# Later turns, copies and second projections, inner values in two parts, and one longer pause per column in a vision tower with a mixture of experts

## The chip, the cores and the metric

The kernel runs on one core of a Trainium2 chip. The metric is the device time of one execution in microseconds, taken as the median of several runs. Engines are named as in the profile: PE is TensorE's matmul stream and PEld its weight loads, DVE is VectorE, ACT is ScalarE, POOL is GpSimd, SP is SyncE, which here only issues DMAs.

## The reference

16 images of 128 x 512 floats are cut into 8 x 8 patches, which makes 1024 tokens of 64 values for each image. Each token is embedded (a 64 x 64 matrix, a bias, a position row), goes through a layer norm and linear attention over 8 heads, and then through a layer norm and 16 experts of which the two best are weighed:

```python
h = _L0_tok_ref(x, W, b, pos_embed)
h = h + _L0_attn_ref(_layernorm(h), Wk, bk, Wq, bq, Wv, bv, Wr, br)
h = h + _L0_ffn_ref(_layernorm(h), gate_w, gate_b, w1, w2, w3)
# the experts, of which the top two count for a token, with weights that sum to one:
h1 = einsum('bsd,edh->bseh', x, w1); h2 = einsum('bsd,edh->bseh', x, w2)   # 64 -> 128 for each expert
hidden = silu(h1) * h2
expert_out = einsum('bseh,eho->bseo', hidden, w3)                          # 128 -> 64
```

All of it is in float32.

## The kernel before

The images are taken as 8 pairs. For a pair, `attend` does the embedding, the attention, the second norm, the choice of experts and the sorting of tokens by expert, cut into stages: a table `PLANS` gives each stage a number k, whole or with a fraction, and `BEGUN` gives the step at which a pair begins (`step_of`). For the experts, POOL scatters the tokens of a pair (twice, once for each of their two experts) as rows of 512 bytes into a DRAM list sorted by expert. The list has 48 tiles of 128 rows, and each tile belongs to one expert. Four tiles are a group, so a pair has 12 groups, and 96 groups g are numbered through all pairs. A group goes through this chain:

- SP loads the rows (`load_rows`), PE turns them (`turn`, four transposes into `turn_ps`), ACT copies them to `rowsT` (also called `turn`, two buffers);
- PE does the first projections (`project_in`, 8 matmuls of 256 columns into `h_ps`, which takes two PSUM banks and has one buffer); the expert of each tile is read into PE registers first (L1144);
- ACT takes the tanh (`activate`), DVE makes the inner values in two steps (`multiply`: `twice`, then `hid`, two buffers);
- PE turns them (`turn_hidden` into `hidT_ps`), ACT copies them (`copy_hidT`, two buffers);
- PE does the second projections (`project_out` into `y_ps`), ACT copies them (`copy_y`, two buffers), SP stores them (`store_y`).

When all rows of a pair are stored, POOL gathers the two rows of each token (`gather`), ACT and DVE weigh and add them (`weigh`, `sum_up`) and SP stores the result.

What sets the order is a loop over steps s that every engine's program has by itself, written out in full. Group g = s - LAG (22) belongs to step s. In step s PE does `project_in(g)`, `turn_hidden(g - 1)`, the stages k of the pairs under way, `turn(g + 1)`, the stages k + 0.5, `project_out(g - 1)` and the stages k + 0.75 (L1174 to L1189). ACT does the stages k, `copy_y(g - 2)`, `activate(g)`, `copy_hidT(g - 1)`, `turn(g + 1)`, the stages k + 0.5 and then the weighing (L643 to L661). DVE does the stages, `multiply(g)`, more stages and sums. Engines wait for each other by counting semaphores only, so one engine may be in another step than the others, but each works its own list strictly in order.

POOL issues 512 indirect DMAs: for each of a pair's 16 columns of 128 tokens two scatters, and later two gathers. A table says in which steps (`SCATTER`, `GATHER`, 6 steps for 16 columns), and at the start of each step POOL waits until PE has turned group g (L526). Ahead of each indirect DMA, `pause` writes 192 zeros per partition into a scratch tile `idle`, and nobody reads them (L477 to L481).

Of the kernel before, what the change touches and what calls it, by code (L numbers as in the profile page):

```python
# [11 lines left out]
ACT = mybir.ActivationFunctionType  # L12
# [50 lines left out]
SCATTER = (16, 22, 29, 43, 56, 69, 82, 95)  # L63
GATHER = (36, 49, 62, 75, 88, 101, 108, 120)
SUMS = [[42 + 14 * m + q for q in range(4)] for m in range(5)] + [[113, 114, 115, 116], [119, 119, 120, 120], [121, 122, 123, 124]]
STORED = 2
# [29 lines left out]

GROUPS_ALL = GROUPS * PAIRS


def vit_kernel(nc, x, tok_w, tok_b, pos, wk, bk, wq, bq, wv, bv, wr, br, gate_w, gate_b, w1, w2, w3, out):  # L100
# [3 lines left out]
    with ExitStack() as ctx:  # L104
# [114 lines left out]

        idle = sb("idle", [P, 192])  # L220
        rows_all = sb("rows_all", [P, 3, GROUP, 2, E])
# [104 lines left out]
        def _(sp):  # L326
# [102 lines left out]
        def _(pool):  # L429
# [53 lines left out]
            def scatter(m, j):  # L483

                n = m % 3
                if j == 0:
                    wait(pool, "place_ready", m + 1)
                    wait(pool, "z_split", m + 1)
                    if m >= 3:
                        wait(pool, "rowsT_ps_ready", GROUPS * (m - 2))  # L490
                    else:
                        pool.wait_ge(rows_zeroed[n], 16)
                for r in range(2):
                    pause()
                    gp.indirect_dma_start(rows_dram[n], bass.IndirectOffsetOnAxis(ap=place[m % RING][:, r, j:j + 1], axis=0),  # L495
                                          z_parts[m % 2][:, j // 2, j % 2, :, :].rearrange("p n e -> p (n e)").bitcast(F32),
                                          None).then_inc(scattered[n], 16)

            def gather(m, j):
# [9 lines left out]
                if j == 0 and apart(m):  # L509
                    wait(pool, "att_ps_ready", 3 * PAIRS)  # L510
                for r in range(2):
                    pause()
                    gp.indirect_dma_start(y_of[r][apart(m)][:, j // 2, j % 2, :], None, y_dram[m % 3],  # L513
                                          bass.IndirectOffsetOnAxis(ap=place[m % RING][:, r, j:j + 1], axis=0)).then_inc(gathered[apart(m)][q], 16)
# [18 lines left out]
        def _(act):  # L533
# [63 lines left out]
            def turn(g):  # L597
                wait(act, "rowsT_ps_ready", g + 1)
                wait(act, "h_done", g - 1)
                sc.activation(rowsT[g % 2][:, :], turn_ps[:, :], ACT.Copy).then_inc(S["rowsT_ready"], 1)  # L600

            def activate(g):
                wait(act, "h_done", g + 1)
                wait(act, "twice_done", g)
                if g == 0:
                    for n in range(3):
                        act.wait_ge(rows_zeroed[n], 16)
                sc.activation(tanh[:, :, :], h_ps[:, :].rearrange("p (j n h) -> p j n h", j=GROUP, n=2)[:, :, 0, :],  # L608
                              ACT.Tanh, scale=0.5).then_inc(S["tanh_done"], 1)

# [32 lines left out]
            for s in range(SPAN):  # L643
                g = s - LAG
                for m, k in steps_at(s):
                    attend(m, k)
                if 0 <= g - 2 < GROUPS_ALL:
                    copy_y(g - 2)
                if 0 <= g < GROUPS_ALL:
                    activate(g)  # L650
                if 0 <= g - 1 < GROUPS_ALL:
                    copy_hidT(g - 1)
                if 0 <= g + 1 < GROUPS_ALL:
                    turn(g + 1)
                for m, k in steps_at(s):
# [8 lines left out]
        def _(dve):  # L664
# [280 lines left out]
            def find_owners(m):  # L945
                wait(dve, "owner_ps_ready", m + 1)
                if m >= 3:
                    wait(dve, "h_done", GROUPS * (m - 2))
                ve.tensor_scalar(owner[m % 3][:, :], sides[second(m)][0:1, 258:258 + TILES], float(EXPERTS - 1), None,
                                 ALU.min).then_inc(S["owner_ready"], 1)  # L950

            def multiply(g):
                wait(dve, "tanh_done", g + 1)
                wait(dve, "hid_done", g)
# [3 lines left out]
                ve.scalar_tensor_tensor(twice[:, :, :], tanh[:, :, :], 1.0, halves[:, :, 0, :], ALU.add, ALU.mult).then_inc(S["twice_done"], 1)  # L958
                wait(dve, "twice_done", g + 1)
                wait(dve, "hidT_ps_ready", g - 1)  # L960
                ve.scalar_tensor_tensor(hid[g % 2][:, :, :], twice[:, :, :], 0.5, halves[:, :, 1, :], ALU.mult, ALU.mult).then_inc(S["hid_done"], 1)  # L961

# [28 lines left out]
        def _(pe):  # L991
# [146 lines left out]
            def project_in(g):  # L1138
# [7 lines left out]
                wait(pe, "rowsT_ready", g + 1)  # L1146
                wait(pe, "hid_done", g)
                for j, e in enumerate(experts[g]):
                    for w, first in ((w_hi, True), (w_lo, False)):
                        mm = te.matmul(h_ps[:, j * 256:(j + 1) * 256], rowsT[g % 2][:, j * P:(j + 1) * P],  # L1150
                                       w[:, bass.ds(e, 1), :, :].rearrange("d a n h -> d (a n h)"), start=first, stop=not first)
                mm.then_inc(S["h_done"], 1)

            def turn_hidden(g):
                wait(pe, "hid_done", g + 1)
                wait(pe, "hidT_ready", g)
# [15 lines left out]
            for s in range(SPAN):  # L1172
# [15 lines left out]
                for m, k in steps_at(s):  # L1188
# [24 lines left out]
```

## Time and profile before

| | |
|---|---|
| median of 3 runs | 1007.12 us (1001.66 to 1008.42) |
| the profiled execution | 997.99 us, span 996.1 us |
| PE, PEld busy | 69%, 57% of the span |
| POOL busy | 66% |
| DVE, ACT busy | 43%, 34% |
| TensorE's granted clock, mean | 0.773 of full |
| POOL's indirect DMAs | 512, 0.95 to 0.99 us each |

Read the shares as means over a start (until about 160 us) in which there are no groups yet, a long middle with attention and groups, a stretch from about 780 us with groups and gathers only, and an end from 941 us in which POOL gathers for the last pair.

### The profile page before, as it was taken

How to read it: one execution, taken by the hardware profiler on the slowest of the kernel's cores; microseconds unless marked ns; L12 is line 12 of the kernel's file. 1: busy time of each engine (PE TensorE's matmuls, PEld its weight loads, DVE VectorE, ACT ScalarE, POOL GpSimd, SP SyncE). 2: the span in 40 equal slices, each digit the busy share in tenths (PEclk: the TensorE clock that was granted, in tenths of full speed). 3: DMA queues.
4: the chain of work that ended last, by engine and by line, in shares of the span. 5: the costliest groups of instructions: out<-in, count | busy, mean ns of one | idle time of the engine just before them, and what ended most of it. 6: DMA issues, size and time to landing. Idle time of an engine off the chain costs nothing.

```text
span 996.1 us, 14389 instructions
## 1 busy us (share of the span) xinstructions
PE 684.5 (69%) x3844; PEld 568.1 (57%) x3844; DVE 427.0 (43%) x1045; ACT 339.2 (34%) x657; POOL 661.8 (66%) x1052
## 2 busy tenths in 40 slices
PE   6866676886778677886777777887659556656500
PEld 3555356765775576565755667577657555545400
DVE  4755534642445544453555264534552221112411
ACT  2231112432342444244443354234432332223611
POOL 1050786848588677848884888757884887586085
PEclk9978767877789878878898787977875767657755
DMA  2991312343321732253335243242422333223221
GB/s 62 169 347 75 102 45 85 91 116 101 88 68 43 173 107 74 60 143 91 104 71 118 81 122 90 48 125 80 108 70 70 92 93 80 69 68 78 58 44 31
DMA packets 168871, 93.20 MB, mean 94 GB/s; under 512 B 99680, under 2 KB 152928, under 8 KB 168800
## 3 DMA queue, kind: packets, MB, share of 16 engines
q1 hardware_dynamic: 151632, 66.71, 25.7%
q0 software_dynamic: 16384, 25.20, 9.3%
q8 instruction: 39, 0.64, 0.3%
q10 hardware_dynamic: 784, 0.39, 0.2%
q14 instruction: 32, 0.26, 0.1%
HBM read 45.06 MB, written 47.19 MB: 93 GB/s over the span
## 4 chain that ended last, share of the span: by engine, by line
PE 41%; another core or an unknown queue 25%; issue 12%; DVE 8%; ACT 6%; POOL 4%; DMA 2%; SPq 0%; ACTq 0%; POOLq 0%; DVEq 0%
PE h_ps L1150 11%; PE y_ps L1167 7%; PE hidT_ps L1160 4%; PE wide_ps L1019 4%; PE turn_ps L1135 4%; POOL sums L513 3%; PE wide_ps L1039 2%; ACT sums L633 1%; ACT hidT_all L616 1%; PE wide_ps L1111 1%; PE side_ps L1086 1%; POOL idle L480 1%; DMA rows_all<-rows_scratch 1%; PE wide_ps L1126 1%
## 5 line engine op out<-in xcount | busy, mean ns | idle before, releaser
L495 POOL DMA_INDIRECT rows_scratch<-z_parts,place x256 | 254.4, 994 | 43.6 <-issue 40.7
L480 POOL MEMSET idle<- 128x192 f32 x512 | 140.2, 274 | 196.4 <-issue 62.9
L513 POOL DMA_INDIRECT sums<-y_scratch,place x224 | 219.0, 978 | 36.6 <-issue 33.3
L1150 PE MATMUL h_ps<-w_hi,rowsT 128*128 x384 | 140.7, 382 | 97.6 <-issue 53.7
L1167 PE MATMUL y_ps<-w_sb,hidT_all 128*128 x768 | 128.5, 320 | 94.5 <-issue 49.8
L1167 PEld LDWEIGHTS y_ps<-w_sb,hidT_all 128*128 128x128 f32 x768 | 118.6, 233 | 113.9 <-issue 113.5
L958 DVE SCALAR_TENSOR_TENSOR twice_y<-tanh,h_ps 128x512 f32<-128x512 f32 x96 | 65.9, 686 | 264.2 <-ACT tanh L608 134.7
L1150 PEld LDWEIGHTS h_ps<-w_hi,rowsT 128*128 128x128 f32 x384 | 97.0, 252 | 113.4 <-issue 112.9
L1150 PE MATMUL h_ps<-w_lo,rowsT 128*128 x384 | 129.8, 352 | 0.0
L600 ACT ACTIVATE rowsT<-turn_ps 128x512 fp32r<-128x512 f32 x96 | 57.5, 599 | 183.3 <-remote 112.8
L608 ACT ACTIVATE tanh<-h_ps 128x512 f32<-128x512 f32 x96 | 57.2, 596 | 164.1 <-remote 78.8
L1150 PEld LDWEIGHTS h_ps<-w_lo,rowsT 128*128 128x128 f32 x384 | 99.9, 260 | 0.1
L1160 PE MATMUL hidT_ps<-ident,hid_all 128*128 128x128 f32 x384 | 81.5, 351 | 1.7 <-issue 1.7
L1135 PE MATMUL turn_ps<-ident,rows_all 128*128 128x128 f32 x384 | 74.3, 323 | 9.6 <-issue 8.4
L621 ACT ACTIVATE twice_y<-y_ps 128x256 f32<-128x256 f32 x96 | 36.7, 383 | 105.4 <-remote 73.4
L1135 PEld LDWEIGHTS turn_ps<-ident,rows_all 128*128 128x128 f32 x384 | 57.9, 172 | 22.3 <-issue 19.7
L961 DVE SCALAR_TENSOR_TENSOR hid_all<-twice_y,h_ps 128x512 f32<-128x512 f32 x96 | 65.9, 686 | 3.3
L616 ACT ACTIVATE hidT_all<-hidT_ps 128x512 f32<-128x512 f32 x96 | 57.2, 596 | 28.5 <-remote 19.1
L1160 PEld LDWEIGHTS hidT_ps<-ident,hid_all 128*128 128x128 f32 x384 | 62.0, 182 | 1.1 <-issue 1.1
L1019 PE MATMUL wide_ps<-w_patch,x_cols 64*128 64x512 f32 x224 | 56.6, 627 | 3.1 <-DVE w_patch L683 3.1
L970 DVE SCALAR_TENSOR_TENSOR sums<-sums,gate 128x64 f32<-128x64 f32 x112 | 24.5, 280 | 78.2 <-ACT sums L633 39.0
L633 ACT ACTIVATE sums<-sums,mean_all,gate 128x64 f32<-128x64 f32 x112 | 39.9, 431 | 39.0 <-DMA sums<-y_scratch,place 39.0
(251 smaller groups left out, 946.3 us busy)
## 6 DMA issues: line engine op xcount, KB each, us to landing
rows_all<-rows_scratch SPq DMA_DIRECT2D x96, 256.0 KB
y_scratch<-twice_y SPq DMA_DIRECT2D x96, 128.0 KB
rows_scratch<-tanh SPq DMA_DIRECT2D x3, 3072.0 KB, 19.4
xi_scratch<-xi SPq DMA_DIRECT2D x16, 256.0 KB
rows_scratch<-z_parts,place POOLq DMA_INDIRECT x256
hx<-xi_scratch SPq DMA_DIRECT2D x14, 256.0 KB
sums<-y_scratch,place POOLq DMA_INDIRECT x224
out<-sums SPq DMA_DIRECT2D x56, 64.0 KB
```

The lines of the kernel that those rows point to most:

```text
L480: gp.memset(idle[:, :], 0.0).then_inc(S["idled"], 1)
L495: gp.indirect_dma_start(rows_dram[n], bass.IndirectOffsetOnAxis(ap=place[m % RING][:, r, j:j + 1], axis=0), z_parts[m % 2][:, j // 2, j % ...
L513: gp.indirect_dma_start(y_of[r][apart(m)][:, j // 2, j % 2, :], None, y_dram[m % 3], bass.IndirectOffsetOnAxis(ap=place[m % RING][:, r, j: ...
L600: sc.activation(rowsT[g % 2][:, :], turn_ps[:, :], ACT.Copy).then_inc(S["rowsT_ready"], 1)
L616: sc.activation(hidT[g % 2][:, :], hidT_ps[:, :], ACT.Copy).then_inc(S["hidT_ready"], 1)
L958: ve.scalar_tensor_tensor(twice[:, :, :], tanh[:, :, :], 1.0, halves[:, :, 0, :], ALU.add, ALU.mult).then_inc(S["twice_done"], 1)
L961: ve.scalar_tensor_tensor(hid[g % 2][:, :, :], twice[:, :, :], 0.5, halves[:, :, 1, :], ALU.mult, ALU.mult).then_inc(S["hid_done"], 1)
L1019: te.matmul(wide_ps[:, b * 512:(b + 1) * 512], x_cols[second(m)][half, j, :], w_patch[half, j, :, :].rearrange("p t e -> p (t e)"), start= ...
L1135: mm = te.transpose(turn_ps[:, j * P:(j + 1) * P], rows[g % 3][:, j, :, :].rearrange("p n e -> p (n e)"), ident[:, :])
L1150: mm = te.matmul(h_ps[:, j * 256:(j + 1) * 256], rowsT[g % 2][:, j * P:(j + 1) * P], w[:, bass.ds(e, 1), :, :].rearrange("d a n h -> d (a ...
L1160: mm = te.transpose(hidT_ps[:, j * P:(j + 1) * P], hid[g % 2][:, j, :], ident[:, :])
L1167: mm = te.matmul(y_ps[:, j * E:(j + 1) * E], hidT[g % 2][:, j * P:(j + 1) * P], w3_sb[:, bass.ds(e, 1), :].rearrange("h a d -> h (a d)"), ...
```

## The change

Six things are changed together. PE turns the rows of group g + 2 instead of g + 1 in a step, and has its second projections of group g - 2 (it was g - 1) ahead of `turn_hidden`, right behind the first ones. ACT begins a step with its three copies, those of `hidT` and `y` a group later than before, and ahead of the stages. Tanh and inner values of a group are made in two halves of two tiles each (`HALVES`), with counts to match, and so are PE's first projections: the second half waits for the second half of the inner values before. SP loads rows three groups ahead and stores three behind. `pause` writes 512 zeros instead of 192 and is called once a column instead of once an indirect DMA. POOL's wait at L526 is not changed in text, but the turn of group g is now done a step earlier. The tables `GATHER` and `SUMS` move some entries by one step.

```diff
-GATHER = (36, 49, 62, 75, 88, 101, 108, 120)
-SUMS = [[42 + 14 * m + q for q in range(4)] for m in range(5)] + [[113, 114, 115, 116], [119, 119, 120, 120], [121, 122, 123, 124]]
+GATHER = (37, 49, 62, 75, 88, 101, 109, 121)
+SUMS = [[42 + 14 * m + q for q in range(4)] for m in range(5)] + [[114, 115, 116, 117], [120, 120, 121, 121], [122, 123, 124, 125]]
+HALVES = (slice(0, GROUP // 2), slice(GROUP // 2, GROUP))
-        idle = sb("idle", [P, 192])
+        idle = sb("idle", [P, 512])
-                if 0 <= g + 2 < GROUPS_ALL:
-                    load_rows(g + 2)
-                if 0 <= g - 2 < GROUPS_ALL:
-                    store_y(g - 2)
+                if 0 <= g + 3 < GROUPS_ALL:
+                    load_rows(g + 3)
+                if 0 <= g - 3 < GROUPS_ALL:
+                    store_y(g - 3)
...
+                pause()
                 for r in range(2):
-                    pause()
                     gp.indirect_dma_start(...)
...
             def activate(g):
-                wait(act, "h_done", g + 1)
-                wait(act, "twice_done", g)
-                sc.activation(tanh[:, :, :], ...)
+                for i, j in enumerate(HALVES):
+                    wait(act, "h_done", 2 * g + i + 1)
+                    wait(act, "twice_done", 2 * g + i - 1)
+                    sc.activation(tanh[:, j, :], ...)
...
                 g = s - LAG
+                if 0 <= g + 1 < GROUPS_ALL:
+                    turn(g + 1)
+                if 0 <= g - 3 < GROUPS_ALL:
+                    copy_y(g - 3)
+                if 0 <= g - 2 < GROUPS_ALL:
+                    copy_hidT(g - 2)
                 for m, k in steps_at(s):
                     attend(m, k)
-                if 0 <= g - 2 < GROUPS_ALL:
-                    copy_y(g - 2)
                 if 0 <= g < GROUPS_ALL:
                     activate(g)
-                if 0 <= g - 1 < GROUPS_ALL:
-                    copy_hidT(g - 1)
-                if 0 <= g + 1 < GROUPS_ALL:
-                    turn(g + 1)
...
             def multiply(g):
+                for i, j in enumerate(HALVES):
+                    wait(dve, "tanh_done", 2 * g + i + 1)
+                    wait(dve, "hid_done", 2 * g + i - 1)
+                    ve.scalar_tensor_tensor(twice[:, j, :], ...)
+                    wait(dve, "twice_done", 2 * g + i + 1)
+                    ve.scalar_tensor_tensor(hid[g % 2][:, j, :], ...)
...
             def project_in(g):
-                wait(pe, "hid_done", g)
-                for j, e in enumerate(experts[g]):
+                for i, half in enumerate(HALVES):
+                    wait(pe, "hid_done", 2 * g + i - 1)
+                    for j in range(half.start, half.stop):
...
                 if 0 <= g < GROUPS_ALL:
                     project_in(g)
+                if 0 <= g - 2 < GROUPS_ALL:
+                    project_out(g - 2)
                 if 0 <= g - 1 < GROUPS_ALL:
                     turn_hidden(g - 1)
                 for m, k in steps_at(s):
                     attend(m, k)
-                if 0 <= g + 1 < GROUPS_ALL:
-                    turn(g + 1)
+                if 0 <= g + 2 < GROUPS_ALL:
+                    turn(g + 2)
                 for m, k in steps_at(s):
                     attend(m, k + 0.5)
-                if 0 <= g - 1 < GROUPS_ALL:
-                    project_out(g - 1)
                 for m, k in steps_at(s):
                     attend(m, k + 0.75)
```

## Rows read from the trace of the kernel before

**Rows 1.** The page, sections 1 and 2: busy time of each engine, and granted clock.

```profile
PE 684.5 (69%) x3844; PEld 568.1 (57%) x3844; DVE 427.0 (43%) x1045; ACT 339.2 (34%) x657; POOL 661.8 (66%) x1052
PEclk9978767877789878878898787977875767657755
```

**Rows 2.** The page, section 4: the chain that ended last, by engine.

```profile
PE 41%; another core or an unknown queue 25%; issue 12%; DVE 8%; ACT 6%; POOL 4%; DMA 2%; SPq 0%; ACTq 0%; POOLq 0%; DVEq 0%
```

**Rows 3.** Stretches: from:to, length; busy PE, PEld, DVE, ACT, POOL; clock, DMA, GB/s.

```profile
547.70:655.90 108.20, 85.43 (x501) 70.33 (x501) 52.60 (x126) 43.16 (x85) 81.33 (x128) 0.82 0.36 94
...
811.70:860.20 48.50, 30.28 (x144) 27.39 (x144) 10.84 (x22) 15.24 (x32) 39.39 (x64) 0.63 0.37 87
915.00:941.00 26.00, 18.98 (x117) 16.54 (x115) 12.00 (x30) 15.17 (x37) 0.00 (x0) 0.83 0.24 61
```

**Rows 4.** Timeline of one group's step without POOL (start, length; idle before it).

```profile
922.72 0.40 PE L1150 MATMUL h_ps<-w_hi,rowsT 128*128 x1 [1.06 <-issue]
...
924.64 0.60 ACT L608 ACTIVATE tanh<-h_ps 128x512 f32<-128x512 f32 x1 [2.16 <-PE h_ps L1150]
...
925.50 0.60 ACT L616 ACTIVATE hidT_all<-hidT_ps 128x512 f32<-128x512 f32 x1 [0.26 <-PE hidT_ps L1160]
...
926.24 1.15 PE L1167 MATMUL y_ps<-w_sb,hidT_all 128*128 x8
...
928.41 0.38 PE L1150 MATMUL h_ps<-w_hi,rowsT 128*128 x1 [1.03 <-issue]
```

**Rows 5.** Timeline of a step with POOL at work.

```profile
841.07 1.10 PE L1167 MATMUL y_ps<-w_sb,hidT_all 128*128 x8 [0.39 <-ACT hidT_all L616]
...
845.70 0.38 ACT L621 ACTIVATE twice_y<-y_ps 128x256 f32<-128x256 f32 x1 [3.03 <-remote]
...
850.03 0.60 ACT L608 ACTIVATE tanh<-h_ps 128x512 f32<-128x512 f32 x1 [3.95 <-remote]
```

**Rows 6.** Waits of the whole span: us in total, times, longest us.

```profile
ACT rowsT L600 <- remote: 112.8, 27, 8.9
ACT tanh L608 <- remote: 78.8, 25, 7.0
ACT twice_y L621 <- remote: 73.4, 19, 6.5
```

**Rows 7.** Groups of instructions: busy us, mean ns of one; idle before them.

```profile
L961 DVE SCALAR_TENSOR_TENSOR hid_all<-twice_y,h_ps 128x512 f32<-128x512 f32 x96 | 65.9, 686 | 3.3
...
L608 ACT ACTIVATE tanh<-h_ps 128x512 f32<-128x512 f32 x96 | 57.2, 596 | 164.1 <-remote 78.8 <-PE h_ps L1150 66.0 <-issue 19.3
...
L816 DVE TENSOR_TENSOR qs<-wide_ps,qmax 128x256 f32<-128x256 f32 x28 | 11.9, 425 | 1.0
...
L572 ACT ACTIVATE vals<-wide_ps 128x256 f32<-128x256 f32 x28 | 10.7, 383 | 37.6 <-DVE qs L816 21.1 <-issue 16.2
```

**Rows 8.** Timeline of the steps ahead of the first group.

```profile
144.44 0.22 PE L1116 MATMUL hidT_ps<-ones,hot_sum 128*16 128x1 f32 x2
...
150.87 6.41 SPq L355 DMA_DIRECT2D rows_all<-rows_scratch  x4
...
155.78 1.06 PE L1135 MATMUL turn_ps<-ident,rows_all 128*128 128x128 f32 x4
...
158.46 0.57 PE L1150 MATMUL h_ps<-w_hi,rowsT 128*128 x1 [1.18 <-ACT rowsT L600]
```

**Rows 9.** Groups of POOL's instructions, the first 512-element zeroing from the setup.

```profile
L513 POOL DMA_INDIRECT sums<-y_scratch,place x224 | 219.0, 978 | 36.6 <-issue 33.3 <-POOL idle L480 3.1
L480 POOL MEMSET idle<- 128x192 f32 x512 | 140.2, 274 | 196.4 <-issue 62.9 <-DVE place L943 40.5 <-PE turn_ps L1135 37.1
...
L440 POOL MEMSET tanh<- 128x512 f32 x1 | 0.5, 518 | 0.0
```

**Rows 10.** Timeline of POOL in the end, the first and last of 32 gathers.

```profile
943.23 0.26 POOL L480 MEMSET idle<- 128x192 f32 x1 [28.31 <-DVE base L970]
943.89 0.95 POOL L513 DMA_INDIRECT sums<-y_scratch,place  x1 [0.40 <-issue]
...
986.97 0.95 POOL L513 DMA_INDIRECT sums<-y_scratch,place  x1 [0.16 <-issue]
```

More of the change, by code:

```diff
@@ L510, in gather @@
                     wait(pool, "att_ps_ready", 3 * PAIRS)
+                pause()
                 for r in range(2):
-                    pause()
                     gp.indirect_dma_start(y_of[r][apart(m)][:, j // 2, j % 2, :], None, y_dram[m % 3],
@@ L598, in turn @@
                 wait(act, "rowsT_ps_ready", g + 1)
-                wait(act, "h_done", g - 1)
+                wait(act, "h_done", 2 * (g - 1))
                 sc.activation(rowsT[g % 2][:, :], turn_ps[:, :], ACT.Copy).then_inc(S["rowsT_ready"], 1)
             def activate(g):
-                wait(act, "h_done", g + 1)
-                wait(act, "twice_done", g)
                 if g == 0:
@@ L607, in activate @@
                         act.wait_ge(rows_zeroed[n], 16)
-                sc.activation(tanh[:, :, :], h_ps[:, :].rearrange("p (j n h) -> p j n h", j=GROUP, n=2)[:, :, 0, :],
-                              ACT.Tanh, scale=0.5).then_inc(S["tanh_done"], 1)
+                for i, j in enumerate(HALVES):
+                    wait(act, "h_done", 2 * g + i + 1)
+                    wait(act, "twice_done", 2 * g + i - 1)
+                    sc.activation(tanh[:, j, :], h_ps[:, :].rearrange("p (j n h) -> p j n h", j=GROUP, n=2)[:, j, 0, :],
+                                  ACT.Tanh, scale=0.5).then_inc(S["tanh_done"], 1)
             def copy_hidT(g):
@@ L947, in find_owners @@
                 if m >= 3:
-                    wait(dve, "h_done", GROUPS * (m - 2))
+                    wait(dve, "h_done", 2 * GROUPS * (m - 2))
                 ve.tensor_scalar(owner[m % 3][:, :], sides[second(m)][0:1, 258:258 + TILES], float(EXPERTS - 1), None,
@@ L952, in multiply @@
             def multiply(g):
-                wait(dve, "tanh_done", g + 1)
-                wait(dve, "hid_done", g)
                 if g == 0:
@@ L957, in multiply @@
                 halves = h_ps[:, :].rearrange("p (j n h) -> p j n h", j=GROUP, n=2)
-                ve.scalar_tensor_tensor(twice[:, :, :], tanh[:, :, :], 1.0, halves[:, :, 0, :], ALU.add, ALU.mult).then_inc(S["twice_done"], 1)
-                wait(dve, "twice_done", g + 1)
                 wait(dve, "hidT_ps_ready", g - 1)
-                ve.scalar_tensor_tensor(hid[g % 2][:, :, :], twice[:, :, :], 0.5, halves[:, :, 1, :], ALU.mult, ALU.mult).then_inc(S["hid_done"], 1)
+                for i, j in enumerate(HALVES):
+                    wait(dve, "tanh_done", 2 * g + i + 1)
+                    wait(dve, "hid_done", 2 * g + i - 1)
+                    ve.scalar_tensor_tensor(twice[:, j, :], tanh[:, j, :], 1.0, halves[:, j, 0, :], ALU.add, ALU.mult).then_inc(S["twice_done"], 1)
+                    wait(dve, "twice_done", 2 * g + i + 1)
+                    ve.scalar_tensor_tensor(hid[g % 2][:, j, :], twice[:, j, :], 0.5, halves[:, j, 1, :], ALU.mult, ALU.mult).then_inc(S["hid_done"], 1)
             def sum_up(m, q):
@@ L1146, in project_in @@
                 wait(pe, "rowsT_ready", g + 1)
-                wait(pe, "hid_done", g)
-                for j, e in enumerate(experts[g]):
[L1149 to L1152, printed above, removed]
+                for i, half in enumerate(HALVES):
+                    wait(pe, "hid_done", 2 * g + i - 1)
+                    for j in range(half.start, half.stop):
+                        for w, first in ((w_hi, True), (w_lo, False)):
+                            mm = te.matmul(h_ps[:, j * 256:(j + 1) * 256], rowsT[g % 2][:, j * P:(j + 1) * P],
+                                           w[:, bass.ds(experts[g][j], 1), :, :].rearrange("d a n h -> d (a n h)"), start=first, stop=not first)
+                    mm.then_inc(S["h_done"], 1)
             def turn_hidden(g):
-                wait(pe, "hid_done", g + 1)
+                wait(pe, "hid_done", 2 * g + 2)
                 wait(pe, "hidT_ready", g)
```

## The prediction

> **What bounds the kernel now.** I read the page first. [...] The chain that ended last is PE for 41%, and another 25% is put down to something that the profile doesn't see [rows 2]. [...] A pair takes 108.2 us with PE busy for 85 of them and POOL for 81; a stretch with groups and gathers only takes 48.5 us for six steps, 8.1 us each, with PE busy for 62% of it; the last stretch without POOL takes 26 us for five steps, 5.2 us each [rows 3].
>
> A step without POOL shows the loop. From the first matmul into `h_ps` to the tanh 1.92 us, tanh and the copy of `hidT` 1.6 us, then the second projections, and 2.17 us from their first matmul to the next first projection, of which 1.03 us is PE reading expert numbers with an empty array [rows 4]. The copy of `hidT` stands behind the tanh on ACT, and `project_out(g - 1)` stands behind that copy and ahead of `project_in(g + 1)` on PE: the ACT link of 1.6 us is in the loop of every step.
>
> A step with POOL at work shows something else. The second projections start at 841.07 and their copy at 845.70, though the eight matmuls are written down with 1.10 us; the tanh comes at 850.03 [rows 5]. The releaser is "remote": PE's signals come 3 to 5 us after its matmuls. In total ACT waits 112.8, 78.8 and 73.4 us in this way for turns, first and second projections, 27, 25 and 19 times in 96 steps [rows 6]. What makes them late I can't read; it goes with POOL's indirect DMAs, since 8.1 - 5.2 = 2.9 us a step is the difference between the two stretches.
>
> **The change part by part.** The sum is made against the profiled run, 998 us, and that stands 9 us below the median shown.
>
> (1) *Second projections a group later, copies first on ACT.* The 1.6 us link leaves PE's loop. What stays in a step is PE's own: 8 + 8 matmuls and 8 transposes, and the 1.03 us of reading. At full clock eight matmuls take 1.1 us less overlap [rows 5], 2.8 us for all 24, so 3.9 us in place of 5.1 (the 5.69 from one first projection to the next, less 0.6, since the first projections shown ran at half clock); at half clock the array alone needs twice 2.8, 5.6 us, and 0.1 is won. With a mean clock of 0.83 [rows 3], two thirds of the time is at full, so 0.66 x 1.2 + 0.34 x 0.1 = 0.8; I take 0.7 us. Steps in which an attention stage holds PE up win nothing, so I count 64 of 96: **-45 us**. Bounds: 0, and 96 x 1.1 = -106.
>
> (2) *Slack for late signals.* `y_done` now has almost a step until ACT asks for it, as has `hidT_ps_ready`. The 73.4 us on L621 are the part that can go. But if PE itself is late and not only its signal, they come back at the next wait, the tanh's, which keeps no slack. I take a third: **-24 us**, bounds 0 and -73. The 112.8 us on the turn's copy I leave at 0 (bound -113): a good part is ACT waiting while PE works on stages.
>
> (3) *The turn two groups ahead, at the start.* In PE's step 20 `turn(0)` now stands between the stages k and k + 0.5. It needs the first row load, issued at 150.87, while the matmul at 144.44 is the first of `rank` for pair 1, which stood ahead of that turn and now stands behind it [rows 8]. `load_rows(0)` moves up on SP as well, but it waits for the same scatters. No row gives the landing: it lies between 150.87 and the turn at 155.78. I take 153.5; with 1.06 us of turn, rank starts at 154.6 in place of 144.44, and the turn leaves its old place: 10.1 - 1.1 = **+9 us**, bounds +6.4 and +11.3. Behind `rank` stand place, scatter of pair 1, the context and group 0, so nothing hides it. Later turns gain slack: their loads are issued a step earlier too, against the same three buffers.
>
> (4) *Halves.* A tanh of 512 columns takes 596 ns, a copy of 256 383: +170 ns on ACT. DVE: four of 425 for two of 686, +328 ns [rows 7]. That is 0.5 us a step, 48 us in all. The cover is PE: between the first half of `h_ps` and the next write to it lie second projections, transposes and register reads, 3.9 us at least, while that half needs 0.4 + 0.4 + 0.4 us. I take **0**, and +48 without cover. [...]
>
> (5) *POOL's pauses.* One indirect DMA comes each (986.97 - 943.89) / 31 = 1.39 us [rows 10], so 2.78 a column. After: 0.52 for 512 zeros [rows 9], 0.16, two DMAs of 0.95 and between them 0 to 0.16: 2.58 to 2.74. If two DMAs in a row can't follow each other faster than now, 3.3. POOL is alone at the end, 16 columns: -3 to +8 us, I take **-1**. Elsewhere POOL follows PE's steps: 64 DMAs of 1.39 us are 89 us of a pair's 108, so it waits, and a wait that comes free a step earlier wins nothing by itself. It is a floor, though: no pair under some 88 us.
>
> (6) *The end.* The second projections of group 94 now stand between `project_in(95)` and the turn of its inner values: 0.85 to 2 us, **+1**. SP: `store_y` is behind one more step but its buffer count is unchanged, and behind it on SP are the loads and stores of the stages, which waited for the same copy before: 0. `GATHER` and `SUMS`: 0, the queues are past their waits there.
>
> Sum: 998 - 45 - 24 + 9 + 0 - 1 + 1 = 938 in the profiled run, and 9 more for the median: **947 us**.
>
> **The rivals.** Forecast (0.57): as summed; own range 905 to 985.
>
> *Large gain* (0.08): the link goes in all steps and late signals hide. Then POOL is the bound, at 88 us a pair: five pairs at 20 us less, and a gather stretch that shrinks a little, with the 9 us of the start: about 890. For it: POOL's 81 busy us a pair. Against it: the tanh's wait has no slack.
>
> *Halves on the path* (0.14): the first projections' second half waits for the second half of `hid`, and on a late signal PE has nothing else left to do; then the 48 us are paid: 995. For it: the tanh waits 78.8 us for signals already. Against: 3.9 us of cover.
>
> *No loop gain* (0.08): the clock stays at half where steps are short, so the array is the bound, and late means PE itself: 998 - 10 + 9 + 9 = 1006.
>
> *Slower* (0.13): POOL's two DMAs directly behind each other make PE's signals later. The place is `pause`, now outside the loop over r. POOL's company costs 2.9 us a step, some 85 steps, 247 us. From a quarter more (+62 us) on it eats the gain of 60; at a third more, 947 + 82 = 1029. For it: steps are quiet only where POOL is. Against it: DMAs per us stay the same.
>
> **Numbers.** A measurement of this kernel can tell about 1%. Faster by more: 0.57 + 0.08 + half of the halves' case, 0.73. Within 1%: the rest of that and most of "no loop gain", 0.11. Slower: 0.16. The range leaves out the lower end of the large gain and most of the slower case: 895 to 1005.
>
> **What would show it.** In the profile after: steps without POOL at 4 to 4.7 us; second projections right behind first ones, with no wait for `hidT_all`; the "remote" wait of L621 mostly gone and that of L608 still there; the first tanh at about 169 us in place of 160.6; a pair at 98 to 102 us; POOL's column at 2.6 to 2.75 us. Wrong if the steps with POOL stay at 8 us (then late means PE itself), if the copy of `rowsT` at the head of ACT's step holds up the tanh behind it, or if POOL's DMAs grow past 1 us.

## The result: 1072 us, 7% slower, where 947 were forecast

The changed kernel takes 1072.46 us (median of 4, 1071.91 to 1079.92) against 1004.39 for the kernel before in the same rounds (1001.23 to 1008.42): ratio 1.069, interval 1.063 to 1.076. (In this document medians take all runs, and ratios with their 95% intervals leave out those marked slow.) The profiled execution has a span of 1070.3 us. The range ended at 1005; the result is outside it and has the other sign.

The page of the changed kernel (busy time, clock, chain by engine and by line), and its groups for the second and the first projections (busy us, mean ns of one; idle us before them):

```profile
PE 685.2 (64%) x3844; PEld 569.7 (53%) x3844; DVE 450.4 (42%) x1237; ACT 335.0 (31%) x753; POOL 652.9 (61%) x796
PEclk9978758688787978789786887887787866686655
...
PE 30%; another core or an unknown queue 21%; issue 12%; ACT 9%; DVE 7%; POOL 3%; DMA 2%; DVEq 1%; ACTq 0%; SPq 0%; POOLq 0%
PE y_ps L1174 7%; PE wide_ps L1025 4%; PE hidT_ps L1167 3%; PE turn_ps L1141 3%; PE h_ps L1157 3%; POOL sums L515 3%; ACT hidT_all L620 2%; ACT sums L637 2%; ACT twice_y L625 2%; DMA rows_all<-rows_scratch 2%; PE side_ps L1092 2%; PE side_p
...
L1174 PE MATMUL y_ps<-w_sb,hidT_all 128*128 x768 | 142.8, 347 | 237.0 <-ACT hidT_all L620 117.2
...
L1157 PE MATMUL h_ps<-w_hi,rowsT 128*128 x384 | 122.1, 343 | 27.3 <-issue 14.8
```

The same two groups in the kernel before:

```profile
L1150 PE MATMUL h_ps<-w_hi,rowsT 128*128 x384 | 140.7, 382 | 97.6 <-issue 53.7
...
L1167 PE MATMUL y_ps<-w_sb,hidT_all 128*128 x768 | 128.5, 320 | 94.5 <-issue 49.8
```

PE's work is that of [rows 1] (685.2 for 684.5 us); what grew is its waiting. PE's share of the chain falls from 41% [rows 2] to 30%. Ahead of `project_out` (L1174, L1167 before) PE is idle for 237.0 us, 94.5 before; ahead of `project_in` for 27.3, 97.6 before. So part of the wait has only moved from the one to the other, but the two together went from 192.1 to 264.3 us, and these 72 us are nearly all of the 74 by which the span grew. ScalarE's copies of `hidT` and `y` are in the chain with 2% each. The waits (us in total, times, longest) say for what:

```profile
PE y_ps L1174 <- ACT hidT_all L620: 117.2, 41, 8.8
ACT vals L574 <- DVE qs L821: 115.1, 31, 19.4
ACT rowsT L602 <- PE turn_ps L1141: 111.8, 29, 10.5
ACT rowsT L602 <- remote: 106.7, 22, 7.6
...
PE y_ps L1174 <- ACT twice_y L625: 72.8, 20, 6.4
ACT tanh L612 <- remote: 57.0, 32, 4.5
```

Against [rows 6]: the remote wait of the copy of `y` is gone, 73.4 us, as I had said; but PE now waits 190 us (117.2 + 72.8) for two copies of ScalarE. Stretches (columns as in [rows 3]), a pair and a stretch with groups and gathers only:

```profile
608.30:727.30 119.00, 85.44 (x502) 69.87 (x502) 55.35 (x152) 42.60 (x98) 80.19 (x97) 0.81 0.34 89
841.30:920.90 79.60, 42.10 (x218) 38.88 (x218) 20.34 (x57) 21.89 (x58) 66.28 (x81) 0.72 0.32 87
```

A pair takes 119.0 us for 108.2, with the same 85.4 us of PE in it. In the second row 218 records of PE, at 24 a group as in [rows 3], make 9.1 steps of 8.8 us, where [rows 3] had 8.1 (an estimate, since some records can be missing). The path is in the timeline of one step of a pair (start, length; idle time before):

```profile
632.17 1.72 PE L1045 MATMUL wide_ps<-proj_qv,hx 128*128 128x256 f32 x4
...
634.40 1.03 PE L1045 MATMUL wide_ps<-proj_qv,hx 128*128 128x256 f32 x4
...
635.07 0.47 PE L1157 MATMUL h_ps<-w_hi,rowsT 128*128 x1
...
639.45 0.42 DVE L818 TENSOR_REDUCE qmax<-wide_ps 128x32 f32<-128x256 f32 x1 [3.13 <-remote]
...
641.64 0.42 DVE L818 TENSOR_REDUCE qmax<-wide_ps 128x32 f32<-128x256 f32 x1 [1.31 <-remote]
...
642.56 0.38 ACT L574 ACTIVATE vals<-wide_ps 128x256 f32<-128x256 f32 x1 [1.81 <-DVE qs L821]
642.84 1.42 ACT L637 ACTIVATE sums<-sums,mean_all,gate 128x64 f32<-128x64 f32 x4
644.16 0.58 ACT L602 ACTIVATE rowsT<-turn_ps 128x512 fp32r<-128x512 f32 x1
644.64 0.37 ACT L625 ACTIVATE twice_y<-y_ps 128x256 f32<-128x256 f32 x1
644.90 0.59 ACT L620 ACTIVATE hidT_all<-hidT_ps 128x512 f32<-128x512 f32 x1
...
645.64 0.68 PE L1174 MATMUL y_ps<-w_sb,hidT_all 128*128 x2 [8.38 <-ACT hidT_all L620]
```

PE ends two blocks of its queries (L1045) at 633.9 and 635.4 and is already at its next first projections at 635.07. DVE, which takes a maximum from each block (`qmax`), starts at 639.45 and 641.64, 5.6 and 6.2 us behind the block's end, and both waits are named "remote". (The profile models the ends of matmuls, but PE's next ones have started.) Behind DVE on ScalarE stand `vals` and `weigh`, the tail of the step, and only behind these the three copies; PE, which has `project_out` near the head of its next step, waits for them for 8.38 us. Before, the copies of `hidT` and `rowsT` stood ahead of the tail: a signal that came late for `vals` didn't hold up the copy that PE needed next.

Where nothing is late, the new order does what it was read to do. Steps without POOL:

```profile
940.18 0.86 ACT L612 ACTIVATE tanh<-h_ps 128x256 f32<-128x256 f32 x2
940.45 1.24 PE L1174 MATMUL y_ps<-w_sb,hidT_all 128*128 x8
...
943.83 0.79 ACT L612 ACTIVATE tanh<-h_ps 128x256 f32<-128x256 f32 x2
944.10 1.10 PE L1174 MATMUL y_ps<-w_sb,hidT_all 128*128 x8
...
947.35 0.88 ACT L612 ACTIVATE tanh<-h_ps 128x256 f32<-128x256 f32 x2
```

From tanh to tanh 3.6 us, where [rows 3] gave 5.2 a step, and no wait ahead of the second projection. They are a handful of the 96 steps.

### The profile page after: what moved, and what is told of

It reads as the page before. It is cut to its first block, busy times and chain, and to the rows that moved or that the text cites. A ratio compares the mean times of both kernels' runs of the same rounds, so it can differ in the third digit from the quotient of the medians.

```text
span 1070.3 us, 14517 instructions
## 1 busy us (share of the span) xinstructions
PE 685.2 (64%) x3844; PEld 569.7 (53%) x3844; DVE 450.4 (42%) x1237; ACT 335.0 (31%) x753; POOL 652.9 (61%) x796
## 4 chain that ended last, share of the span: by engine, by line
PE 30%; another core or an unknown queue 21%; issue 12%; ACT 9%; DVE 7%; POOL 3%; DMA 2%; DVEq 1%; ACTq 0%; SPq 0%; POOLq 0%
PE y_ps L1174 7%; PE wide_ps L1025 4%; PE hidT_ps L1167 3%; PE turn_ps L1141 3%; PE h_ps L1157 3%; POOL sums L515 3%; ACT hidT_all L620 2%; ACT sums L637 2%; ACT twice_y L625 2%; DMA rows_all<-rows_scratch 2%; PE side_ps L1092 2%; PE side_ps L1071 1%; ACT rowsT L602 1%; PE wide_ps L1087 1%
## 5 line engine op out<-in xcount | busy, mean ns | idle before, releaser
L1174 PE MATMUL y_ps<-w_sb,hidT_all 128*128 x768 | 142.8, 347 | 237.0 <-ACT hidT_all L620 117.2
L482 POOL MEMSET idle<- 128x512 f32 x256 | 138.5, 541 | 244.8 <-issue 87.1
L1174 PEld LDWEIGHTS y_ps<-w_sb,hidT_all 128*128 128x128 f32 x768 | 128.9, 254 | 253.7 <-issue 252.8
L965 DVE SCALAR_TENSOR_TENSOR twice_y<-tanh,h_ps 128x256 f32<-128x256 f32 x192 | 80.2, 418 | 205.2 <-issue 105.9
L1157 PE MATMUL h_ps<-w_hi,rowsT 128*128 x384 | 122.1, 343 | 27.3 <-issue 14.8
L1157 PE MATMUL h_ps<-w_lo,rowsT 128*128 x384 | 109.0, 308 | 0.4 <-issue 0.3
L1157 PEld LDWEIGHTS h_ps<-w_hi,rowsT 128*128 128x128 f32 x384 | 84.0, 219 | 39.0 <-issue 37.9
L612 ACT ACTIVATE tanh<-h_ps 128x256 f32<-128x256 f32 x192 | 69.9, 398 | 92.7 <-remote 57.0
L1157 PEld LDWEIGHTS h_ps<-w_lo,rowsT 128*128 128x128 f32 x384 | 84.0, 219 | 1.2 <-issue 0.9
L967 DVE SCALAR_TENSOR_TENSOR hid_all<-twice_y,h_ps 128x256 f32<-128x256 f32 x192 | 80.8, 421 | 6.6
L1167 PE MATMUL hidT_ps<-ident,hid_all 128*128 128x128 f32 x384 | 80.6, 350 | 0.0
L1167 PEld LDWEIGHTS hidT_ps<-ident,hid_all 128*128 128x128 f32 x384 | 65.0, 206 | 0.0
L574 ACT ACTIVATE vals<-wide_ps 128x256 f32<-128x256 f32 x28 | 10.7, 383 | 107.1 <-DVE qs L821 102.8
```

Of the source, the lines that this page charges most:

```text
L482: gp.memset(idle[:, :], 0.0).then_inc(S["idled"], 1)
L612: sc.activation(tanh[:, j, :], h_ps[:, :].rearrange("p (j n h) -> p j n h", j=GROUP, n=2)[:, j, 0, :], ACT.Tanh, scale=0.5).then_inc(S["ta ...
L965: ve.scalar_tensor_tensor(twice[:, j, :], tanh[:, j, :], 1.0, halves[:, j, 0, :], ALU.add, ALU.mult).then_inc(S["twice_done"], 1)
L967: ve.scalar_tensor_tensor(hid[g % 2][:, j, :], twice[:, j, :], 0.5, halves[:, j, 1, :], ALU.mult, ALU.mult).then_inc(S["hid_done"], 1)
L1167: mm = te.transpose(hidT_ps[:, j * P:(j + 1) * P], hid[g % 2][:, j, :], ident[:, :])
L1174: mm = te.matmul(y_ps[:, j * E:(j + 1) * E], hidT[g % 2][:, j * P:(j + 1) * P], w3_sb[:, bass.ds(e, 1), :].rearrange("h a d -> h (a d)"), ...
```

## Experiments

**Theory T:** the loss is the place of the second projections in PE's order against that of the copies in ScalarE's. **Rival P:** POOL's two DMAs back to back. **Rival H:** the halves. "Late signals" below are waits named "remote"; "the three waits" are those of [rows 6], which add up to 265.0 us in the kernel before.

Later on T is split: T1 says that the new order loses by itself, T2 that it only makes late signals dearer. L says that signals come late as long as POOL's pauses are short, N that the number of pauses or the DMAs back to back count. S says that late signals are a condition of the place and the moment.

### One part at a time

`pauses_only`, the kernel before with

```diff
-                for r in range(2):
-                    pause()
+                pause()
+                for r in range(2):
```

and `idle` of 512; `order_only`, all of the change but halves and pauses; `halves_only`; and `out_at_end`, the changed kernel with one move:

```diff
                     project_in(g)
-                if 0 <= g - 2 < GROUPS_ALL:
-                    project_out(g - 2)
...
                     attend(m, k + 0.5)
+                if 0 <= g - 2 < GROUPS_ALL:
+                    project_out(g - 2)
```

> The kernel before with the new pauses alone: 512 zeros once a column instead of 192 zeros ahead of each of its two DMAs. Theory T (TensorE's second projections, now at the head of its step, wait for ScalarE's copies): nothing of T is in here, so 1004 us within 10. Rival P (GpSimd's two DMAs back to back make the signals of the other engines later, the slower case of the prediction): it carries the loss, 1030 to 1070 us, and TensorE's and ScalarE's idle time without a named cause grows. The remote waits of the copy of y and of the tanh (73.4 and 78.8 us before) tell P directly: unchanged under T, above 90 us each under P.

> The changed order and its tables alone (turns two groups ahead, copies a step later at the head of ScalarE's step, second projections of group g-2 right behind the first of g), with whole inner values and the old pauses. Theory T: nearly the whole loss is here, 1055 to 1075 us, with over 150 us of TensorE's idle time ahead of the second projection, released by the copies of hidT and of y. Rivals P and H (halves): the loss is not here, 1000 to 1010 us.

> The kernel before with the tanh, the two products and the first projection in two halves of 4 rows each; order, tables and pauses as before. Theory T: 1000 to 1010 us (my term for the halves was 0). Rival H (each half pays a signal between engines, and the first half waits for nothing less): up to 48 us more, 1040 to 1055 us, the tanh to product to turn chain of a step longer by 0.7 us or more.

> The changed kernel with one edit: the second projection of group g-2 stands at the end of TensorE's step, behind the turn of group g+2 and the attention's stages k+0.5, instead of right behind the first projection. ScalarE's copy of hidT of g-2 then has TensorE's whole step to be made. Theory T: idle time ahead of the second projection falls from 237 us to under 100 and most of the loss is back, 985 to 1020 us. Rivals P and H: they are all still in it, 1060 to 1075 us.

Measured, with before at 987.7 in the same rounds: pauses alone 961.8 us (0.973, 0.964 to 0.982); order alone 1075.2 (1.090, 1.083 to 1.097); halves alone 1004.1 (1.016, 1.008 to 1.024); the move 1001.5 (1.016, 1.005 to 1.027). The intervals of the pauses, the halves and the move exclude 1, but not an effect under 2%. PE's waits with the order alone, and then with the move:

```profile
PE y_ps L1171 <- ACT hidT_all L619: 121.4, 51, 8.1
```

```profile
L1167 PE MATMUL hidT_ps<-ident,hid_all 128*128 128x128 f32 x384 | 80.0, 346 | 176.6 <-ACT hidT_all L620 138.1
...
PE hidT_ps L1167 <- ACT hidT_all L620: 138.1, 48, 5.8
...
ACT twice_y L625 <- PE y_ps L1174: 29.6, 26, 4.4
```

The order alone loses 87 us, more than the whole change, and one place in it carries most: with `project_out` at the end of PE's step the ratio falls from 1.069 (in other rounds) to 1.016, though PE still waits for the same copy of `hidT`, now ahead of the next turn into `hidT_ps`. PE's idle time ahead of first projections, turns of inner values and second projections is 14.3 + 176.6 + 1.0 = 192 us there, what it was before. P is refuted with its sign: the new pauses are the part that helps, which T had not expected either (about 1004). H is a small cost, 16 us (8 to 24 by the interval). The parts add up: -26 + 87 + 16 = +77 us, where the whole change had +68. The moved entries of `GATHER` and `SUMS` and SP's later loads and stores were never run apart; `out_at_end` has them too, and beyond the pauses and the halves it costs only 1001.5 - 961.8 - 16 = 24 us, so they can't hold more.

### The copies ahead of ScalarE's tail

`copies_early`, the changed kernel with ScalarE's order as (the `if` lines are left out)

```diff
-                    turn(g + 1)
-                    copy_y(g - 3)
-                    copy_hidT(g - 2)
                 for m, k in steps_at(s):
                     attend(m, k)
...
                     activate(g)
+                    copy_y(g - 2)
+                    copy_hidT(g - 1)
+                    turn(g + 2)
```

and `early_whole_start`, the same with whole inner values, group 0 turned one group ahead only and group 1 at the end of that step.

> The changed kernel with one edit on ScalarE: its copies of y (g-2), of hidT (g-1) and of rowsT (g+2) stand right behind the tanh of their step, ahead of the attention's stages k+0.5 and the weighing, instead of one step later at the head of the next. TensorE's order is that of the changed kernel. Theory T (the second projection at the head of TensorE's step is fine by itself; what makes it wait is that the copies come behind ScalarE's tail): TensorE's idle time ahead of the second projection falls from 237 us to under 60 and the whole time is 0.92 to 0.97 of before's, better than with the second projection moved to the end of the step (0.984 to 1.016). Rival (the second projection at the head waits for TensorE's own late signals wherever the copies stand): above 1.00 of before's.

> The kernel of the copies ahead of the tail, with whole inner values instead of halves, and with group 0 turned one group ahead (as in before) so that TensorE's attention stages at the start don't stand behind the rows of group 0; group 1 is turned at the end of the same step. From the parts: the halves alone cost 16 us (ratio 1.016), the early turn of group 0 8.5 us at the first tanh (169.0 against 160.6). Expected 15 to 25 us below the kernel with the copies early alone, 0.91 to 0.95 of before's; first tanh at 158 to 163 us. If the halves cost nothing where TensorE isn't held by copies, only 5 to 10 us below.

1019.5 us (1.017, 1.013 to 1.022) and 1019.8 (1.012, 1.006 to 1.018). With the copies early PE's idle time ahead of `project_out` fell from 237.0 to 82.4 us, not under 60. Most of the loss is back, as with the move of `project_out`, but the expected gain (0.92 to 0.97) is not there: the time is in the range that the rival gave. ScalarE's late signals are longer in sum:

```profile
ACT rowsT L602 <- remote: 109.1, 36, 8.8
ACT twice_y L625 <- remote: 103.1, 42, 4.0
...
ACT tanh L612 <- remote: 69.6, 42, 5.4
```

They are 282 us against 164 in the changed kernel. Moving the copies away from the tail mends PE's wait and puts ScalarE back behind PE's signals. The second kernel's first tanh is at 162.4 us (expected 158 to 163), yet it isn't faster than the first: 15 to 25 us were expected. My reading is that it is not the place of one copy that decides, but how many signals from PE are waited for in a row while they are late; no run isolates that.

### The pauses and the late signals

`pauses_double`, the kernel before with 512 zeros ahead of each DMA (`idle` of 512, nothing else); `no_pauses`, before without `pause()`; then 256 and 320 zeros ahead of each.

> The kernel before with 512 zeros ahead of each indirect DMA (before: 192). The pauses alone (512 once a column) made before faster, 0.973, and ScalarE's longest waits without a named cause fell from 7.0 to 3.2 us for the tanh and from 6.5 to 3.8 us for the copy of y. Theory L (the signals of TensorE come late until GpSimd is off its DMAs for about half a microsecond, so the pause's length counts): with a pause of 0.54 us every 1.7 us the longest of these waits are under 2.2 us and their sums under half of before's; GpSimd's column takes 3.3 us instead of 2.8, some 0.5 us on 480 / 2 columns that partly lie beside idle time, so the whole is 0.95 to 1.01. Theory N (it is the number of pauses or the DMAs back to back that matter): waits as in before, 1.01 to 1.06.

> The kernel before without the zeros between GpSimd's indirect DMAs. Theory L: late signals find no pause within a run of DMAs, so ScalarE's waits without a named cause grow: longest above 10 us, sums of those of rowsT, tanh and y above 350 us (before 265.0), time 1.05 to 1.3 of before's though GpSimd's column is 0.6 us shorter. Theory N (pauses only cost GpSimd's time): 0.95 to 1.00.

> The kernel before with 256 zeros ahead of each indirect DMA (192 in before). If signals get through once the pause is long enough, there is a length between 192 zeros (0.44 us between two DMAs, ScalarE's waits without a named cause 265.0 us) and 512 (0.70 us, none). Here about 0.50 us between DMAs. Threshold below that: no such waits, GpSimd's column 2.9 us, 0.92 to 0.95 of before's. Threshold above: waits as before, 0.99 to 1.02.

> The same with 320 zeros, about 0.54 us between DMAs, GpSimd's column 3.0 us. Threshold below that: no waits without a named cause, 0.93 to 0.96 of before's. Threshold above: they are still there, 0.98 to 1.02.

With 512 zeros each 981.7 us (0.980, 0.976 to 0.985, with before at 1002.4) and not one remote wait left on any engine: L holds here, and N is out. Its page has a chain of another kind, and ScalarE's group of the tanh waits for PE by name:

```profile
POOL 77%; issue 9%; PE 7%; DVE 3%; DMA 2%; ACT 1%; POOLq 0%; ACTq 0%
...
L608 ACT ACTIVATE tanh<-h_ps 128x512 f32<-128x512 f32 x96 | 57.1, 595 | 108.3 <-PE h_ps L1150 81.4 <-issue 26.7
```

No pauses: 1034.9 (1.031, 1.025 to 1.038), the tanh's remote wait 92.5 us, longest 7.5. That is less bad than L expected, and the sum of the three waits is 206 us, not above 350 and even below the 265.0 with 192 zeros, though the kernel is slower. POOL itself now has 64 us of such waits and ScalarE's copy of `hidT` 35.6. So the sum of these waits doesn't measure what they cost. 256 zeros: 989.2 (0.982, 0.975 to 0.990), faster than expected (0.99 to 1.02) with 246 us in the three waits; before ran at 1007.6 in these rounds. 320: 969.6 (0.961, 0.953 to 0.968; 0.98 to 1.02 expected), where the waits nearly keep their sum, 242 us (the 251.8 in a later expectation has a fourth wait in it), and get short:

```profile
ACT rowsT L600 <- remote: 116.0, 47, 6.3
...
ACT tanh L608 <- remote: 70.8, 40, 3.3
...
ACT twice_y L621 <- remote: 55.3, 38, 3.3
```

The longest of tanh and `y` are 3.3 us here, 7.0 and 6.5 in [rows 6], and 3.2 and 3.8 with 512 zeros once a column. So from 192 zeros up the length of the pause counts: longer ones cut the delays short, and somewhere between 0.54 us from the end of a DMA to the next (320 zeros) and 0.70 (512) they go altogether. Whether the time without a DMA does it or the zeroing itself was not separated.

### The changed kernel without late signals

> The changed kernel with 512 zeros ahead of each indirect DMA. With this pause the kernel before has no wait left without a named cause at all (0 us against 265.0 us on ScalarE), and TensorE's signals come in time. Theory T1 (the order of the change loses by itself: TensorE waits for copies that stand behind ScalarE's tail, late signals or not): the whole is 50 us or more above the kernel before with the same pauses (0.980 of before's), 1.03 or more, and over 120 us idle ahead of the second projection. Theory T2 (the order puts more handoffs between TensorE and ScalarE in a row, and only late signals make them dear): without late signals the second projection waits under 80 us and the whole is bound by GpSimd's pauses as there, 0.97 to 1.00.

990.9 us (0.983, 0.976 to 0.990), against 981.7 (0.980) for the same pauses in the old order in other rounds. No remote wait is left here either. T1 with its 50 us is out; a smaller cost of the order could hide here, since POOL is the bound. PE's wait is there, but smaller:

```profile
PE y_ps L1174 <- ACT hidT_all L620: 71.7, 43, 7.8
```

### Where before itself runs at 844 us

> The kernel before with 384 zeros ahead of each indirect DMA, about 0.60 us between two DMAs (0.54 us with 320 zeros, where ScalarE's waits without a named cause were still 251.8 us; 0.70 us with 512, where there were none). GpSimd's column about 3.1 us. Threshold at or below 0.60 us: none of those waits, the time falls towards GpSimd's own, 0.93 to 0.96 of before's. Threshold above: waits as with 320, and 0.95 to 0.98.

> The same with 448 zeros, about 0.65 us between two DMAs, column about 3.2 us. Threshold below: no waits without a named cause, 0.95 to 0.98 of before's, bound by GpSimd as with 512 (0.980). Threshold above: those waits still over 150 us, 0.95 to 0.98 as well; the waits tell it, not the time.

> The changed kernel with 384 zeros ahead of each DMA. Theory T2 (the loss is the order of the change times late signals): if signals are in time at this pause, it stands within 2% of the kernel before with the same pauses; if they are still late, it is 4% or more above that kernel and the second projection waits over 150 us. Theory T1 (the order loses by itself): 4% or more above it either way.

> The kernel with ScalarE's copies ahead of its tail, whole inner values, group 0 turned as late as in before, and 448 zeros ahead of each DMA. Where no signal is late, a step without attention stages takes 3.6 us in the changed order against 5.2 us in before's, and the start is not behind. Theory T2 expects it at least as fast as the kernel before with 448 zeros: 0.94 to 0.98 of before's; the last tanh earlier by 10 us or more. If it is bound by GpSimd alone, the two are the same within 0.5%.

In these rounds the kernel before ran at 844.5 us (7 runs, 841 to 846), not at about 1000; the numbers can only be read with that. 384 zeros: 924.3 us (1.096, 1.093 to 1.100); 448: 951.9 (1.128, 1.123 to 1.133); the changed kernel with 384: 936.5 (1.110, 1.106 to 1.113); the early order with 448: 953.4 (1.130, 1.127 to 1.134). None of the four has a remote wait. So they place no threshold, but they show a floor: there the time goes with POOL's columns. From one DMA to the next but one, a column, takes 2.78 us in before, 3.09 with 384 zeros and 3.20 with 448, and there are 256 columns: 0.31 x 256 = 79 us more and 0.42 x 256 = 108, measured 79.9 and 107.4.

The changed order against the old one with 384 zeros costs 12 us, 1.3%: within the 2% of T2, and T1 wanted 4% or more. POOL's timeline has them (first the old order, then the new), at the second pair's scatter:

```profile
159.35 0.42 POOL L480 MEMSET idle<- 128x384 f32 x1 [5.24 <-PE turn_ps L1135]
```

```profile
170.92 0.42 POOL L482 MEMSET idle<- 128x384 f32 x1 [15.22 <-PE turn_ps L1141]
```

That is 11.6 us, the early turn of group 0 again: with group 0 turned late, as in the early order with 448 zeros, this wait is 5.48 us, against 5.46 in the old order. In the steps behind, the new order can win nothing, since POOL doesn't follow PE any more. With 448 zeros the early order has its last tanh at 842.8 us, the old at 854.5, and the two end within 0.2%. T2 expected the first; the second is what was named for POOL as the bound, not the gain that T2 allowed.

> The kernel before, unchanged, for a profile beside its times. In the call before this one it ran at 844 us (7 runs, 841 to 846) where it had run at 985 to 1008 us in all calls before. Theory S (the late signals of TensorE are a condition of the place and the moment, not of the kernel): where it runs at about 844 us its profile has no wait of ScalarE without a named cause, 108 us or less of TensorE's idle time there, and GpSimd's columns of 2.8 us make the chain; where it runs at about 1000 us those waits are 250 us or more, as in the trace of before. Rival (something else is faster at 844 us: the clock, the DMAs): the waits without a cause are there at both times.

> The changed kernel, unchanged, on the same chip in the same rounds. Theory T2 (the loss is the order of the change times the late signals): where before runs at about 844 us, the changed kernel has no late signals either and stands within 5% of it, 850 to 885 us: GpSimd's column is 2.93 us instead of 2.79, 0.14 us on some 240 columns or 34 us where they bind, less what the shorter steps give back. Theory T1 (the order loses by itself): 900 to 920 us. Where before runs at about 1000 us: 1060 to 1080 us, as in the result.

Before ran at about 990 us here: 994.8 us for the copy, with 226 us in the three waits of [rows 6]. That was expected to be 250 or more; the profile at 844 us that would have tested S was not had. The changed kernel took 1023.4 (1.034, 1.021 to 1.046), below the 1060 to 1080 expected. So the size of the loss is not fixed, 3% to 7% where signals are late; its sign was the same in both.

> The kernel before with 384 zeros ahead of each indirect DMA (0.60 us between two DMAs), once more, beside runs of before. Where before runs at about 1000 us (late signals): the waits without a named cause either are gone, and the time is then that of the same kernel where before ran at 844 us, 920 to 930 us or 0.92 to 0.94 of before's, and the threshold lies between 0.54 and 0.60 us; or they are still above 150 us, and the time is 0.94 to 0.97 of before's. Where before runs at 844 us again: 924 us, as before, and nothing new on the threshold.

Before at 848.3 again, 384 zeros 926.7 (1.091, 1.086 to 1.095): nothing new on the threshold.

### The sum over all of them

With the floor, 844.5 us plus 256 times what a column is longer than 2.78, and 14 for the early turn of group 0 (POOL's idle time ahead of the zeros, 60.4 us against 46.3 in the two kernels with 384 zeros), each kernel splits into POOL's part and the rest. The columns are typical distances in POOL's timelines; the rest is worked out, not measured apart, and it takes for granted that before at 844.5 us stands on the floor:

| kernel | column, us | floor | measured | above it |
|---|---|---|---|---|
| before, in the rounds of its parts | 2.78 | 844 | 988 | 143 |
| pauses only | 2.91 | 878 | 962 | 84 |
| 320 zeros each | 2.98 | 896 | 970 | 74 |
| 512 zeros each | 3.30 | 978 | 982 | 4 |
| no pauses | 2.50 | 773 | 1035 | 262 |
| order only | 2.78 | 858 | 1075 | 217 |
| changed kernel | 2.91 | 892 | 1072 | 181 |
| the same, 512 zeros each | 3.31 | 994 | 991 | -3 |

The two levers cross: longer pauses raise the floor and take away late signals, and the new order makes what is left of them dearer, 217 for 143 with the old pauses and 181 for 84 with the new (132 where it took 1023.4; the rounds differ by as much as the kernels here, so only the order of the sizes is shown).

## Why the prediction was wrong

**Step (1), the second projections a group later, -45 us: this failed.** It says that "the ACT link of 1.6 us" leaves PE's loop. In quiet steps it does, and by more (3.6 us a step, 4 to 4.7 expected). But with late signals PE came to wait 190 us for the two copies, and its idle time ahead of first and second projections rose from 192 to 264 us. I looked at the copy's distance in groups and not at what stands between: at the head of ScalarE's step the copy of `hidT` is behind the whole tail of the step before, `vals`, `kT` and `weigh`, and its reader is near the head of PE's. I named the tail nowhere. The order alone costs 87 us (1.090) instead of giving 60. My own line, "if the copy of `rowsT` at the head of ACT's step holds up the tanh behind it", was the right place and the wrong victim: held up are the copies and the second projection. The full and the half clock of this step's sum are in the trace of before: 1.00 from 928.41 to 930.00 us, 0.50 from 923.12 to 926.00. Four turns of inner values take 0.44 us at the full (929.56 to 930.00) and 0.84 at the half (924.41 to 925.25), six first projections 0.82 and 1.29; that all of the 2.8 us doubles was an estimate.

**Step (2), slack for late signals, -24:** the wait of L621 went as said, from 73.4 us to nothing, and that of the tanh stayed (57.0). But a wait of 190 us took its place on PE. I had written that "they come back at the next wait, the tanh's"; they came back through another engine, by way of DVE's and ScalarE's part of the attention. The sign of being wrong that I had named, "if the steps with POOL stay at 8 us", came as well (8.8 by PE's records). "Then late means PE itself" doesn't follow, though: the query blocks above had ended, and PE was at work on its next matmuls, while DVE still waited.

**Step (3), the start, +9:** right. First tanh at 169.0 us (about 169 expected), PE 12.9 us idle for the row load ahead of the turn. Without late signals it costs 12 to 14.

**Step (4), halves, 0 (or +48):** 16 us when alone, between my ends and nearer to the one I took. In `halves_only` DVE's busy time rose by 22.7 us and ScalarE's by 15.7 (449.7 and 354.9 us, from 427.0 and 339.2 in [rows 1]), 38.4 us together, where the sum has 48.

**Step (5), pauses, -1:** wrong twice. The column came to 2.91 us, not 2.58 to 2.74: from the end of the first DMA to the start of the second 0.30 us pass without a zero between them, so this gap shrank by only 0.14 us (from 0.44), while the other grew by 0.26 (from 0.44 to 0.70). And this edit alone gives 26 us, and the longest waits of tanh and `y` fell from 7.0 and 6.5 us to 3.2 and 3.8; the trace of before held one length of pause only and could not show it. The slower rival had this place with the wrong sign.

**Step (6)** was too small to be seen. Pairs at 98 to 102 us were expected, they are 119. The chance of 0.73 for faster was too high (its terms add up to 0.72): the case that happened, a new wait of PE for ScalarE, was none of my rivals.

## What to carry to other kernels

When a consumer is moved to the head of an engine's step, list all that its producer's engine does between the old reader's time and the new, the tail of the last step first; a distance in steps is no slack if both ends move. Ask of every wait for "remote" what a late signal would hold up behind it, and keep what another engine needs ahead of such a wait. And where one engine's pauses set how late the others' signals come, sweep their length first: it was worth more here (0.961 with 320 zeros) than any order, but only where signals are late. Where before ran at 844 us, 384 zeros cost 9% (320 were not run there), so no version here is shown to be faster in both conditions.

## What the hardware showed that I had not expected

- PE's signals are waited for, for up to 8.9 us [rows 6], while POOL issues indirect DMAs 0.30 to 0.54 us apart, and not at all at 0.70 us throughout (no remote wait, where before has 265 us in three). With 0.30 and 0.70 us in turn (pauses once a column) 213 us are left. The stretches without POOL have none (914 to 941 us in before, 936 to 947 in the changed kernel). The mean granted clock doesn't tell the two apart: 0.787 with none (512 zeros), 0.80 with many (320 zeros, profiled run).
- The same kernel ran at about 1000 us in most rounds and at 844 to 848 in two sets of them, on one chip at both levels (987.7 and 844.5). By the length of POOL's columns its late signals are missing there, but no profile of the kernel before was taken there. The granted clock is higher there as well, 0.836 for 0.776, as cause or as consequence; no run tells. What brings the one or the other is open; both times every kernel beside it had 384 zeros or more ahead of each DMA, which was so in no other rounds and may be chance.
- With no zeros between them two indirect DMAs follow each other 0.30 us apart from end to start, never closer; 192 zeros (274 ns) add 0.14 us only, to 0.44.
